# Second LayerNorm of a fused two-layer graph kernel: its row statistics by bn_stats and bn_aggr on VectorE instead of sums on VectorE and squares on ScalarE

## The chip, the cores and the metric

The kernel runs on one core of one Trainium2 chip. The metric is the device time of one execution in microseconds; lower is better. Five engines run their own queues in order and meet at semaphores: TensorE (PE; PEld for its weight loads), VectorE (DVE), ScalarE (ACT), GpSimd (POOL) and SyncE (SP), which issues the DMAs.

## The reference, cut to what matters

```python
# x: (128, 64, 512), adj: (64, 64); weights 512 x 512
def _L1_gnn_ref(h, causal_mask, ...):          # causal_mask = adj
    z_l, z_g, v = h @ W_lang.T, h @ W_grav.T, h @ W_V.T
    zn = z_l / max(norm(z_l), EPS)
    A_l = max(zn @ zn.T, 0) * not_eye
    A_g = exp(-d2(z_g) / (2 * sigma**2)) * not_eye
    K = w_l * row_stochastic(A_l * adj) + (1 - w_l) * row_stochastic(A_g * adj)
    return (K @ v) @ W_O.T
x = _layernorm(x + adj-mixed x + bias)
x = _layernorm(x + _L1_gnn_ref(x, adj, ...))   # the LayerNorm whose statistics change
```

`_layernorm` is (x - mean) / sqrt(var + 1e-5) over the last axis.

## The kernel before

The 128 graphs are worked on in 16 groups of 8. A group is 512 rows, held as four tiles (pairs) of 128 rows x 512 columns, and a name with an index p (`residual(g, p)`) works on one of them. Each engine runs one function `iteration`, once per group, in a fixed order written out by hand: the first group alone, a hardware loop over the next twelve, and the last three alone. What stands in an iteration belongs to several groups at once: the projections of group g (`project`, `diagonal_blocks`, `values`), the Gram matrices of g (`gram`), the attention output of the group before (`attend`, `residual`, the second LayerNorm and the store), the first layer of the next one (`mix`, `add_bias`, `row_stats`, `norm_rows`, `h_high`, `h_low`), and the scaling and splitting of the input of the one after that (`x_scaled`, `x_high`, `x_low`) and of the third (`x_squares`, `x_sum`, `x_base`).

Products run in fp16 with each operand split into a high and a low part. ScalarE makes the high parts (`p_hi`, `u_hi` in `uv`, `h_hi`, `x_hi`, `ks_hi`, `kt_hi`), and VectorE or GpSimd the low ones by subtraction (`p_lo`, `u_lo`, `h_lo`, `x_lo`, `ks_lo`, `kt_lo`).

Names and lines that matter below:

- TensorE: `attend_gate` (L609) is a small matmul in front of `attend` (L628) that carries its waits, among them for `kt_lo` (L1045). `gram` (L552) writes `ps_t`, the four `values` (L538) follow, then `third_norm` (L465), and then `spread` (L567), which needs both halves of `r_sb`: `shifted` (L1064) and `diagonal_matrices` (L1069). `symmetrise` (L576, L578) comes behind it.
- From `ps_t` to `r_sb`: ScalarE copies `t_sb` (`t_copy`, L799), GpSimd makes `t_diag` (L1463), VectorE sums it (`diagonals`, L1056) and scales it (`squared_norms`, nsq, L1060), GpSimd raises it to the power -1/2 (`inverse_norm`, rr, L1469), and VectorE builds `r_sb` from `rr` (L1069).
- GpSimd also subtracts two of the four `h_lo` (L1438, pairs 2 and 3) and all `x_lo` (L1433).
- Second LayerNorm: `residual` (L1120) writes `o` and, as an accumulator output, its row sum `osum`. `out_means` (L1128) turns two sums at a time into `omean`. On ScalarE `o_squares` (L829) squares o plus the mean, and its accumulator is the variance `ovar`. GpSimd's `ln2` (L1446, L1448) makes `rstd2`, VectorE's `out_shift` (L1132) `nmr2`, and ScalarE's `normalise` (L834) writes the output, which SyncE stores.
- `norm_rows` (L1030) overwrites the `h` tile that the residual of the same pair has read, and therefore waits for `sum_ready`, which `residual` raises.
- The last group's statistics (`back`, L1160 on) are bn_stats already.

Of the kernel before, what the change touches and what calls it, by code (L numbers as in the profile page):

```python
# [29 lines left out]
P = 128  # L30
# [28 lines left out]
def resnorm_graph_kernel(nc, x, adj, bias, w_lang, w_grav, w_v, w_o, gate, log_sigma, out):  # L59
# [20 lines left out]
    with ctx:  # L80
# [46 lines left out]
        osum = sb("osum", [P, PAIRS])  # L127
        omean = sb("omean", [P, PAIRS])
        ovar = sb("ovar", [P, PAIRS])
        o_square = sb("o_square", [P, PAIRS, D], BF16)  # L130
# [172 lines left out]
        omean_ready = sem("omean_ready")  # L303
        ovar_ready = sem("ovar_ready")
# [457 lines left out]
        def _(act):  # L762
# [85 lines left out]
            def iteration(g, has_prev, has_next, has_split, has_square):  # L848
# [8 lines left out]
                if has_split and not first:  # L857
                    x_scaled(split, 0)
                    x_scaled(split, 1)
# [4 lines left out]
                if has_split and not first:  # L864
                    x_high(split, 0)
                if has_prev:
                    ks_high(before)
# [3 lines left out]
                if has_split and not first:  # L871
                    x_scaled(split, 2)
                p_high(g, 3, first)
                if first:
                    for p in range(PAIRS):
                        x_scaled(split, p)
                if has_prev:
                    kt_high(before)
                if has_split and not first:
                    x_high(split, 1)  # L880
                p_high(g, 4, first)
                p_high(g, 5, first)
                if has_square:
                    x_squares(third, 0)
                p_high(g, 6, first)
# [4 lines left out]
                if has_next:  # L890
                    if has_square:
                        x_squares(third, 1)
                        x_squares(third, 2)
                    h_high(nxt, 0)
                    if has_prev:
                        u_high(g, 0)
                    if has_split and not first:
                        x_high(split, 2)
                    h_high(nxt, 1)
                    t_copy(g, first)  # L900
                    if first:
                        u_high(g, 0)
                    if has_square:
                        x_squares(third, 3)
                    h_high(nxt, 2)
                    if has_split and not first:
                        x_scaled(split, 3)
                    h_high(nxt, 3)
                    u_high(g, 1)
                    if has_prev:  # L910
                        o_squares(before, 0)
                        o_squares(before, 1)
                        o_squares(before, 2)
                        o_squares(before, 3)
                    u_high(g, 2)
                    if has_split and not first:
                        x_high(split, 3)
                    rectify(g)
# [7 lines left out]
                else:  # L926
                    t_copy(g, False)
                    o_squares(before, 0)
                    o_squares(before, 1)
                    o_squares(before, 2)  # L930
                    o_squares(before, 3)
# [59 lines left out]
        def _(dve):  # L991
# [124 lines left out]
            def residual(g, p, first):  # L1116
                dve.wait_ge(ku_done, g.count(2, p // 2 + 1))
                if p == 0 and not first:
                    dve.wait_ge(o_moved, g.prev().count(16, 32))
                dve.scalar_tensor_tensor(out=o[:, p, :], in0=ku_bank[p][:, :], scalar=ku_scale[:, 0:1],  # L1120
                                         in1=h[g.parity][:, p, :], op0=ALU.mult, op1=ALU.add,
                                         accum_out=osum[:, p:p + 1]).then_inc(sum_ready, 1)

            def out_means(g, half):

                pairs = slice(2 * half, 2 * half + 2)
                dve.wait_ge(sum_ready, g.count(4, 2 * half + 2))
                dve.tensor_scalar(omean[:, pairs], osum[:, pairs], -(D ** -1.5), None, ALU.mult).then_inc(omean_ready, 1)  # L1128

            def out_shift(g):  # L1130
                dve.wait_ge(rstd2_ready, g.count(1, 1))
                dve.scalar_tensor_tensor(out=nmr2[:, :], in0=omean[:, :], scalar=D ** 0.5, in1=rstd2[:, :],  # L1132
# [27 lines left out]
            def back(g):  # L1160
# [15 lines left out]
                def moments(half):  # L1176
                    dve.wait_ge(stats2_ready, 2 * half + 2)
# [28 lines left out]
            def iteration(g, has_prev, has_next, has_split, has_square):  # L1206
# [7 lines left out]
                if has_prev:  # L1214
                    gravities(before)
                    u_low(before, 3)
                    row_sums(before)
                if has_next:
                    add_bias(nxt, 1)
                if has_prev:  # L1220
                    scaled_sums(before)
                    clamped_sums(before)
                if has_next:
                    row_stats(nxt, 0)
                if has_prev:
                    inverse_sums(before)
                    row_factors(before)
# [5 lines left out]
                if has_prev:  # L1233
                    scale_rows(before)
# [4 lines left out]
                if has_prev:  # L1239
                    rows_low(before)  # L1240
                p_low(g, 2)
                if has_next:
                    add_bias(nxt, 2)
                    add_bias(nxt, 3)
                p_low(g, 3)
                if has_next:
                    row_stats(nxt, 2)
# [12 lines left out]
                p_low(g, 6)  # L1260
                p_low(g, 7)
                if has_next:
                    norm_rows(nxt, 0, before)
                    if has_prev:
                        residual(before, 1, False)
                    norm_rows(nxt, 1, before)
# [4 lines left out]
                    h_low(nxt, 0)  # L1271
                    if has_prev:
                        residual(before, 2, False)
                    h_low(nxt, 1)
                    norm_rows(nxt, 2, before)
                    if has_prev:
                        residual(before, 3, False)
                    norm_rows(nxt, 3, before)
                    if has_prev:
                        u_low(g, 0)  # L1280
# [274 lines left out]
```

## Time and profile before

| | us |
|---|---|
| median of three runs | 575.25 |
| the three runs | 574.25, 577.51, 575.25 |
| the profiled execution | 577.62 |
| its span, from first to last instruction | 575.8 |
| TensorE busy in the span | 551.4 (96%) |
| VectorE, ScalarE, GpSimd busy | 466.9, 388.9, 210.8 |
| granted TensorE clock, mean | 0.991 |

All durations in this document come from the profiled execution. A duration in a row runs from start to finish; consecutive operations overlap at their ends, so that the distance between two starts (called the pitch below) is up to 0.1 us shorter. An idle time stands in brackets behind the instruction that it precedes, with what released it.

### The profile page before, as it was taken

The page shows a single profiled execution, that of the slowest core. Times are in us where ns is not written, and L with a number is a line of the kernel's source. Part 1 is how long each engine was busy: PE and PEld are TensorE (multiplying, and loading weights), DVE is VectorE, ACT ScalarE, POOL GpSimd, SP SyncE. Part 2 cuts the span into 40 slices and gives each one's busy share as a digit, 9 for nine tenths or more (in the row PEclk, how much of TensorE's full clock was granted, in tenths as well). Part 3 has the DMA queues.
Part 4 walks back from the last instruction along what each step waited for, and adds up shares of the span by engine and source line. Part 5 has one row for each costly group of instructions (what it writes and reads, how often), then busy time and mean ns, then how long its engine had stood idle before and what let it go on. Part 6 is the DMA issues. An engine that isn't in the chain of part 4 may idle for free.

```text
span 575.8 us, 16176 instructions
## 1 busy us (share of the span) xinstructions
PE 551.4 (96%) x6280; PEld 290.9 (51%) x6280; DVE 466.9 (81%) x1009; ACT 388.9 (68%) x794; POOL 210.8 (37%) x230
## 2 busy tenths in 40 slices
PE   9989789999999999999999999999999999999893
PEld 6544544645454545546454545455464545454361
DVE  1676878798897979797988979797979989896645
ACT  2577736778687677777786876777767866636362
POOL 0132442625244252626152442526262534313021
PEclk9999899999999999999999999999999999999998
DMA  8764161565634435454535344354545332414103
GB/s 247 221 142 90 38 119 42 79 168 67 166 63 130 88 95 127 87 146 96 146 69 154 64 125 98 85 138 87 146 95 146 64 106 38 133 26 88 60 2 146
DMA packets 94845, 60.81 MB, mean 106 GB/s; under 512 B 73184, under 2 KB 75232, under 8 KB 94816
## 3 DMA queue, kind: packets, MB, share of 16 engines
q1 hardware_dynamic: 94816, 60.42, 44.4%
q8 instruction: 19, 0.31, 0.2%
q14 instruction: 10, 0.08, 0.0%
HBM read 21.27 MB, written 16.78 MB: 66 GB/s over the span
## 4 chain that ended last, share of the span: by engine, by line
PE 82%; SPq 6%; DVE 5%; DMA 4%; issue 1%; ACT 1%; POOL 0%; POOLq 0%; ACTq 0%; DVEq 0%
PE proj L538 21%; PE proj L497 18%; PE ps_t L552 8%; PE ps_k L538 7%; PE ps_k L497 6%; PE proj L508 4%; PE front L459 3%; PE ps_v L567 3%; PE ps_t L576 3%; PE ps_k L508 2%; SPq L361 2%; DMA o<-in_L_gnn_W_O 2%; PE ps_t L628 2%; PE front L628 2%; SPq L372 1%
## 5 line engine op out<-in xcount | busy, mean ns | idle before, releaser
L1433 POOL TENSOR_TENSOR x_lo<-x_in,x_hi 128x512 f16<-128x512 f32 x60 | 70.1, 1180 | 158.3 <-ACT x_hi L778 158.3
L538 PE MATMUL proj<-m_hi,ht_hi 128*64 128x512 f16 x384 | 73.8, 381 | 0.0
L538 PE MATMUL proj<-m_hi,ht_lo 128*64 128x512 f16 x384 | 73.4, 379 | 0.0
L538 PE MATMUL proj<-m_lo,ht_hi 128*64 128x512 f16 x384 | 73.4, 379 | 0.0
L1050 DVE TENSOR_TENSOR p_lo<-proj,p_hi 128x512 f16<-128x512 f32 x96 | 63.0, 683 | 9.1 <-ACT p_hi L788 8.0
L788 ACT ACTIVATE p_hi<-proj 128x512 f16<-128x512 f32 x96 | 53.4, 597 | 20.1 <-PE proj L508 20.1
L497 PE MATMUL proj<-ht_lo,l_lang_hi 128*128 128x512 f16 x144 | 54.7, 380 | 2.2 <-DMA ht_lo<-h_lo 1.7
L552 PE MATMUL ps_t<-ht_hi,p_hi 128*128 128x64 f16 x512 | 48.9, 196 | 3.8 <-DVE p_lo L1050 3.8
L1463 POOL TENSOR_TENSOR t_diag<-t_sb,eye 128x512 f32<-128x512 f32 x15 | 19.7, 1310 | 87.4 <-ACT t_sb L799 87.4
L782 ACT ACTIVATE h_hi<-h 128x512 f16<-128x512 f32 x64 | 39.5, 624 | 18.1 <-DVE h L1030 17.9
L552 PEld LDWEIGHTS ps_t<-ht_hi,p_hi 128*128 128x128 f16 x512 | 46.2, 100 | 10.5 <-issue 6.3
L1030 DVE TENSOR_SCALAR h<-y,mv,rstd 128x512 f32<-128x512 f32 x64 | 46.9, 739 | 4.3 <-POOL rstd L1421 1.4
L552 PE MATMUL ps_t<-ht_lo,p_hi 128*128 128x64 f16 x512 | 48.7, 196 | 0.0
L552 PE MATMUL ps_t<-ht_hi,p_lo 128*128 128x64 f16 x512 | 48.7, 196 | 0.0
L508 PE MATMUL proj<-ht_turn,l_turn 64*64 64x512 f16 x288 | 47.3, 380 | 0.0
L552 PEld LDWEIGHTS ps_t<-ht_lo,p_hi 128*128 128x128 f16 x512 | 46.3, 100 | 0.7 <-issue 0.7
L552 PEld LDWEIGHTS ps_t<-ht_hi,p_lo 128*128 128x128 f16 x512 | 46.3, 100 | 0.0
L834 ACT ACTIVATE o<-o,nmr,rstd 128x512 f32<-128x512 f32 x60 | 44.1, 803 | 1.2 <-DVE nmr L1132 0.8
L999 DVE SCALAR_TENSOR_TENSOR y<-front,xinv,bias_b 128x512 f32<-128x512 f32 x60 | 43.1, 739 | 0.2 <-PE front L459 0.2
L829 ACT ACTIVATE o_square<-o,omean 128x512 bf16<-128x512 f32 x60 | 42.5, 710 | 0.0
L1018 DVE BATCH_NORM_STATS2 stats<-y 128x6 f32<-128x512 f32 x64 | 42.1, 682 | 0.0
L772 ACT ACTIVATE x_in<-x_in,xscale 128x512 f32<-128x512 f32 x60 | 41.3, 714 | 0.0
(272 smaller groups left out, 1614.2 us busy)
## 6 DMA issues: line engine op xcount, KB each, us to landing
x_in<-in_x SPq DMA_DIRECT2D x32, 512.0 KB, 7.1
out<-o SPq DMA_DIRECT2D x15, 1024.0 KB, 5.1
ht_turn<-ht_hi SPq DMA_DIRECT2D x16, 192.0 KB, 2.6
ht_turn<-ht_hi SPq DMA_DIRECT2D x16, 128.0 KB, 2.4
w_raw_lang<-in_L_gnn_W_lang SPq DMA_DIRECT2D x4, 256.0 KB, 3.6
o<-in_L_gnn_W_O SPq DMA_DIRECT2D x1, 1024.0 KB, 10.8
w_raw_grav<-in_L_gnn_W_grav SPq DMA_DIRECT2D x4, 256.0 KB, 10.9
uv<-in_L_gnn_W_V SPq DMA_DIRECT2D x1, 1024.0 KB, 15.3
```

Of the source, the lines that this page charges most:

```text
L497: pe.matmul(unit_bank[j][:, :], a[s][:, blk(k, c), :], b[g.parity][:, k, :], start=(n == 0), stop=False, skip_group_check=True)
L508: return pe.matmul(unit_bank[4 * side + c][cols, :], w, x, start=False, stop=True, skip_group_check=True)
L538: mm = pe.matmul(value_bank[p][q * N:(q + 1) * N, :], a[g.parity][:, k, rows:rows + N], b[:, k, :], start=(n == 0), stop=(n == len(passes) ...
L552: mm = pe.matmul(ps_t[:, b * N:(b + 1) * N], a[:, c, b, :, :].rearrange("p s n -> p (s n)"), t[g.parity][:, c, b * N:(b + 1) * N], start=( ...
L788: act.activation(p_hi[:, j % 4, :, j // 4, :], by_batch(unit_bank[j]), ACT.Copy).then_inc(phi_ready, 1)
L829: act.activation(o_square[:, p, :], o[:, p, :], ACT.Square, scale=D ** -0.5, bias=omean[:, p:p + 1], accum_out=ovar[:, p:p + 1]).then_inc( ...
L834: act.activation(o[:, p, :], o[:, p, :], ACT.Identity, scale=rstd2[:, p:p + 1], bias=nmr2[:, p:p + 1]).then_inc(out_ready, 1)
L999: dve.scalar_tensor_tensor(out=y[:, MIXED[p], :], in0=front[p % 2][:, :], scalar=xinv[g.parity][:, 0:1], in1=bias_b[:, :], op0=ALU.mult, o ...
L1018: dve.bn_stats(stats1[:, MIXED[p], :], y[:, MIXED[p], :]).then_inc(stats1_ready, 1)
L1030: dve.tensor_scalar(h[g.parity][:, p, :], y[:, p, :], mv1[:, p, 0:1], rstd1[:, p:p + 1], ALU.subtract, ALU.mult).then_inc(h_ready, 1)
L1050: dve.tensor_tensor(p_lo[:, j % 4, :, j // 4, :], by_batch(unit_bank[j]), p_hi[:, j % 4, :, j // 4, :], ALU.subtract).then_inc(plo_ready, 1)
L1433: pool.tensor_tensor(x_lo[:, p, :], x_in[g.parity][:, p, :], x_hi[:, p, :], ALU.subtract).then_inc(xlo_ready, 1)
```

## The change

The second LayerNorm of all groups but the last gets its statistics as the last group has them. `residual` no longer writes row sums; one `bn_stats` per pair (`out_stats`) reads `o`, and four `bn_aggr` (`out_moments`) make mean and variance. A tiny operation (`hold`) stands between them, as in the first LayerNorm. `out_means` and `o_squares` go. `ln2` and `out_shift` read `mv2`.

```diff
@@ ScalarE @@
-            def o_squares(g, p):
-                act.wait_ge(omean_ready, g.count(2, p // 2 + 1))
-                act.activation(o_square[:, p, :], o[:, p, :], ACT.Square, scale=D ** -0.5, bias=omean[:, p:p + 1],
-                               accum_out=ovar[:, p:p + 1]).then_inc(ovar_ready, 1)
@@ VectorE @@
                 dve.scalar_tensor_tensor(out=o[:, p, :], in0=ku_bank[p][:, :], scalar=ku_scale[:, 0:1],
-                                         in1=h[g.parity][:, p, :], op0=ALU.mult, op1=ALU.add,
-                                         accum_out=osum[:, p:p + 1]).then_inc(sum_ready, 1)
-
-            def out_means(g, half):
-
-                pairs = slice(2 * half, 2 * half + 2)
-                dve.wait_ge(sum_ready, g.count(4, 2 * half + 2))
-                dve.tensor_scalar(omean[:, pairs], osum[:, pairs], -(D ** -1.5), None, ALU.mult).then_inc(omean_ready, 1)
+                                         in1=h[g.parity][:, p, :], op0=ALU.mult, op1=ALU.add).then_inc(sum_ready, 1)
+
+            def out_stats(g, p):
+                dve.wait_ge(sum_ready, g.count(4, p + 1))
+                dve.bn_stats(stats2[:, p, :], o[:, p, :]).then_inc(stats2_ready, 1)
+
+            def out_moments(g):
+                dve.wait_ge(stats2_ready, g.count(4, 4))
+                dve.tensor_scalar(hold[:, :], stats2[:, 0, 0:1], 1.0, None, ALU.mult)
+                for p in range(PAIRS):
+                    dve.bn_aggr(mv2[:, p, :], stats2[:, p, :]).then_inc(mv2_ready, 1)
@@ GpSimd, ln2 @@
-                pool.wait_ge(ovar_ready, g.count(4, 4))
-                pool.tensor_tensor(ve2[:, :], ovar[:, :], eps_ln[:, :], ALU.add).then_inc(ve2_ready, 1)
...
+                inverse_std(g, mv2_ready, mv2, ve2_ready, ve2, rstd2_ready, rstd2)
@@ GpSimd, iteration @@
                 inverse_norm(g)
+                if has_split and not first:
+                    x_low(split, 2)
                 if has_prev:
                     ln2(before)
                 if has_square:
                     x_scale(third)
                     x_back(third)
-                if has_split and not first:
-                    x_low(split, 2)
```

The hand-written orders change with it. On VectorE, ahead of `kt_low`:

```diff
                 if has_prev:
                     gravities(before)
                     u_low(before, 3)
+                if has_next:
+                    add_bias(nxt, 1)
+                if has_prev:
                     row_sums(before)
...
+                if has_prev:
+                    inverse_sums(before)
+                    row_factors(before)
                 p_low(g, 0)
...
+                if has_prev:
+                    scale_rows(before)
                 p_low(g, 1)
+                p_low(g, 2)
+                if has_next:
+                    add_bias(nxt, 2)
                 if has_prev:
                     rows_low(before)
...
                     add_bias(nxt, 3)
+                    row_stats(nxt, 2)
                 p_low(g, 3)
```

Behind the last projections, norm, residual and low parts alternate otherwise: `norm_rows(0)`, `p_low(7)`, `residual(1)`, `h_low(0)`, `norm_rows(1)`, `residual(2)`, `residual(3)`, `norm_rows(2)`, `h_low(1)`, `norm_rows(3)`. No `norm_rows` stands right behind the residual of its own pair any more. `x_inverse` moves behind `similarities`. On ScalarE the input's work (`x_scaled`, `x_high`, `x_squares`) moves: among others the first `x_high` comes behind `p_high(2)`, `x_scaled(1)` ahead of it, and `ks_high` behind it.

VectorE in the loop, from behind the fourth `norm_rows` to `r_sb` from `rr`; register rows are arithmetic of the queue. Before:

```order
L1040 TENSOR_TENSOR uv<-ps_k,uv 128x512
L1128 TENSOR_SCALAR omean<-osum 128x2
L1056 TENSOR_REDUCE diag<-t_diag 128x8
L1060 TENSOR_SCALAR nsq<-diag,eps_nsq 64x8
L1003 REGISTER_ALU
L1005 TENSOR_REDUCE xsum<-xssq 128x1
L1128 TENSOR_SCALAR omean<-osum 128x2
L1064 TENSOR_TENSOR r_sb<-t_sb,diag 64x512
L1039 REGISTER_ALU
L1040 TENSOR_TENSOR uv<-proj0,uv 128x512
L1069 TENSOR_TENSOR r_sb<-eye2,rr 64x512
```

After:

```order
L1105 BN_STATS stats2<-o 128x6
L1019 REGISTER_ALU
L1020 TENSOR_TENSOR uv<-ps_k,uv 128x512
L1036 TENSOR_REDUCE diag<-t_diag 128x8
L1105 BN_STATS stats2<-o 128x6
L1040 TENSOR_SCALAR nsq<-diag,eps_nsq 64x8
L1105 BN_STATS stats2<-o 128x6 x2
L983 REGISTER_ALU
L985 TENSOR_REDUCE xsum<-xssq 128x1
L1044 TENSOR_TENSOR r_sb<-t_sb,diag 64x512
L1049 TENSOR_TENSOR r_sb<-eye2,rr 64x512
```

Ahead of the shift (the `r_sb` from `t_sb`) stand four bn_stats in place of two omeans, and between it and the second `r_sb` the subtraction of `uv` is gone; two of them now stand behind.

GpSimd at the same place, before and after:

```order
L1463 TENSOR_TENSOR t_diag<-t_sb,eye2 128x512
L1437 REGISTER_ALU
L1438 TENSOR_TENSOR h_lo<-h1,h_hi 128x512 x2
L1469 TENSOR_TENSOR rr<-nsq,minus_half 64x8
L1445 REGISTER_ALU
L1446 TENSOR_TENSOR ve2<-ovar,eps_ln 128x4
L1448 TENSOR_TENSOR rstd2<-ve2,minus_half 128x4
```

```order
L1453 TENSOR_TENSOR t_diag<-t_sb,eye2 128x512
L1430 REGISTER_ALU
L1431 TENSOR_TENSOR h_lo<-h1,h_hi 128x512 x2
L1459 TENSOR_TENSOR rr<-nsq,minus_half 64x8
L1426 TENSOR_TENSOR x_lo<-x_in0,x_hi 128x512
L1411 REGISTER_ALU
L1412 TENSOR_TENSOR ve2<-mv2,eps_ln 128x4
L1414 TENSOR_TENSOR rstd2<-ve2,minus_half 128x4
```

An `x_lo` of 128 x 512 elements now stands right behind `rr`, where the two small operations of the second LayerNorm stood.

VectorE in the last group, before and after:

```order
L1056 TENSOR_REDUCE diag<-t_diag 128x8
L1060 TENSOR_SCALAR nsq<-diag,eps_nsq 64x8
L1064 TENSOR_TENSOR r_sb<-t_sb,diag 64x512
L1040 TENSOR_TENSOR uv<-ps_k,uv 128x512
L1069 TENSOR_TENSOR r_sb<-eye2,rr 64x512
L1040 TENSOR_TENSOR uv<-proj0,uv 128x512
L1132 SCALAR_TENSOR_TENSOR nmr2<-omean,rstd2 128x4
```

```order
L1036 TENSOR_REDUCE diag<-t_diag 128x8
L1040 TENSOR_SCALAR nsq<-diag,eps_nsq 64x8
L1044 TENSOR_TENSOR r_sb<-t_sb,diag 64x512
L1105 BN_STATS stats2<-o 128x6 x2
L1109 TENSOR_SCALAR hold<-stats2 128x1
L1111 BN_AGGR mv2<-stats2 128x2 x4
L1020 TENSOR_TENSOR uv<-ps_k,uv 128x512
L1049 TENSOR_TENSOR r_sb<-eye2,rr 64x512
L1020 TENSOR_TENSOR uv<-proj0,uv 128x512
L1115 SCALAR_TENSOR_TENSOR nmr2<-mv2,rstd2 128x4
```

Two bn_stats, the hold and four bn_aggr now stand between the shift and the first `uv`, and so ahead of the second `r_sb`.

## Rows read from the trace of the kernel before

**Rows 1.** The page's first part: busy us (share of the span), instructions.
```profile
PE 551.4 (96%) x6280; PEld 290.9 (51%) x6280; DVE 466.9 (81%) x1009; ACT 388.9 (68%) x794; POOL 210.8 (37%) x230
```

**Rows 2.** Windows: one loop period, us, busy us of each engine, clock, DMA.
```profile
223.62:255.38 31.76, 31.60 (x384) 16.47 (x385) 27.92 (x60) 23.89 (x51) 13.34 (x15) 1.00 0.46 109
```

**Rows 3.** Timeline of PE: start us, us, engine, line, operation, [idle before <-releaser].
```profile
238.34 0.38 PE L538 MATMUL proj<-m_hi,ht_lo 128*64 128x512 f16 x2
238.65 0.18 PE L465 MATMUL front<-xsum,ones 128*128 128x1 bf16 x1
238.69 1.10 PE L567 MATMUL ps_v<-r_sb,w_spread 128*128 128x512 f32 x2
...
254.84 0.38 PE L508 MATMUL proj<-ht_hi,l_grav_lo 64*64 64x512 f16 x1
255.38 0.17 PE L609 MATMUL ps_v<-ones 128*128 128x1 bf16 x1 [0.16 <-DVE kt_lo L1045]
```

**Rows 4.** Groups by line: the squares on ScalarE, busy us, mean ns | idle.
```profile
L829 ACT ACTIVATE o_square<-o,omean 128x512 bf16<-128x512 f32 x60 | 42.5, 710 | 0.0
```

**Rows 5.** Timeline of DVE in the same period.
```profile
227.90 0.08 DVE L1120 DVE_READ_ACCUMULATOR o<-front,ku_scale,h 128x1 f32 x1
228.02 0.55 DVE L1030 TENSOR_SCALAR h<-y,mv,rstd 128x512 f32<-128x512 f32 x1
...
231.48 0.08 DVE L1120 DVE_READ_ACCUMULATOR o<-ps_v,ku_scale,h 128x1 f32 x1
231.67 1.42 DVE L1030 TENSOR_SCALAR h<-y,mv,rstd 128x512 f32<-128x512 f32 x1
...
233.62 0.52 DVE L1128 TENSOR_SCALAR omean<-osum 128x2 f32<-128x2 f32 x1
...
234.76 0.49 DVE L1060 TENSOR_SCALAR nsq<-diag,eps_nsq 64x8 f32<-64x8 f32 x1
...
237.00 0.68 DVE L1069 TENSOR_TENSOR r_sb<-eye,rr 64x512 f32<-64x512 f32 x1 [0.17 <-POOL rr L1469]
```

**Rows 6.** Timeline of POOL beside it.
```profile
231.54 1.27 POOL L1463 TENSOR_TENSOR t_diag<-t_sb,eye 128x512 f32<-128x512 f32 x1 [6.08 <-ACT t_sb L799]
232.77 2.46 POOL L1438 TENSOR_TENSOR h_lo<-h,h_hi 128x512 f16<-128x512 f32 x2
235.33 1.63 POOL L1469 TENSOR_TENSOR rr<-nsq,minus_half 64x8 f32<-64x8 f32 x1
```

**Rows 7.** Timeline of DVE up to L609, then of POOL beside ks_lo.
```profile
241.55 0.68 DVE L1076 TENSOR_TENSOR a_sb<-e_sb,ps_v 64x512 f32<-64x512 f32 x1 [1.42 <-ACT e_sb L803]
...
249.70 1.23 DVE L1114 TENSOR_TENSOR ks_lo<-ks_sb,ks_hi 128x512 f16<-128x512 f32 x1 [0.23 <-ACT ks_hi L813]
...
253.37 1.27 DVE L1018 BATCH_NORM_STATS2 stats<-y 128x6 f32<-128x512 f32 x2
...
254.74 0.41 DVE L1045 TENSOR_TENSOR kt_lo<-ps_v,kt_hi 128x256 f16<-128x256 f32 x1
255.07 0.37 DVE L1023 BATCH_NORM_AGGREGATE mv<-stats 128x2 f32<-128x6 f32 x4
...
249.22 1.16 POOL L1433 TENSOR_TENSOR x_lo<-x_in,x_hi 128x512 f16<-128x512 f32 x1 [7.07 <-ACT x_hi L778]
```

**Rows 8.** Timeline of DVE, then POOL, in the first group.
```profile
73.69 1.55 DVE L1064 TENSOR_TENSOR r_sb<-t_sb,diag 64x512 f32<-64x512 f32 x1
...
72.41 2.27 POOL L1438 TENSOR_TENSOR h_lo<-h,h_hi 128x512 f16<-128x512 f32 x2 [2.35 <-ACT h_hi L782]
```

**Rows 9.** Timeline of DVE, then PE, in the last group.
```profile
552.74 0.69 DVE L1064 TENSOR_TENSOR r_sb<-t_sb,diag 64x512 f32<-64x512 f32 x1
...
554.96 0.68 DVE L1069 TENSOR_TENSOR r_sb<-eye,rr 64x512 f32<-64x512 f32 x1
...
555.29 0.38 PE L538 MATMUL proj<-m_hi,ht_lo 128*64 128x512 f16 x2
555.74 1.10 PE L567 MATMUL ps_v<-r_sb,w_spread 128*128 128x512 f32 x2
```

More of the change, by code:

```diff
@@ L871, in iteration @@
                 if has_split and not first:
-                    x_scaled(split, 2)
+                    x_scaled(split, 1)
+                    x_high(split, 0)
+                if has_prev:
+                    ks_high(before)
                 p_high(g, 3, first)
@@ L876, in iteration @@
                         x_scaled(split, p)
+                if has_split and not first:
+                    x_high(split, 1)
                 if has_prev:
                     kt_high(before)
-                if has_split and not first:
-                    x_high(split, 1)
                 p_high(g, 4, first)
                 p_high(g, 5, first)
+                p_high(g, 6, first)
                 if has_square:
                     x_squares(third, 0)
-                p_high(g, 6, first)
+                    x_squares(third, 1)
                 p_high(g, 7, first)
@@ L890, in iteration @@
                 if has_next:
-                    if has_square:
-                        x_squares(third, 1)
-                        x_squares(third, 2)
                     h_high(nxt, 0)
+                    if has_split and not first:
+                        x_scaled(split, 2)
                     if has_prev:
@@ L1220, in iteration @@
                 if has_prev:
-                    scaled_sums(before)
-                    clamped_sums(before)
+                    row_sums(before)
                 if has_next:
@@ L1225, in iteration @@
                 if has_prev:
-                    inverse_sums(before)
-                    row_factors(before)
+                    scaled_sums(before)
+                    clamped_sums(before)
                 if has_next:
@@ L1260, in iteration @@
                 p_low(g, 6)
+                if has_next:
+                    norm_rows(nxt, 0, before)
                 p_low(g, 7)
                 if has_next:
-                    norm_rows(nxt, 0, before)
                     if has_prev:
                         residual(before, 1, False)
+                    h_low(nxt, 0)
                     norm_rows(nxt, 1, before)
@@ L1304, in iteration @@
                     residual(before, 3, False)
-                    out_means(before, 0)
-                    out_means(before, 1)
+                    out_stats(before, 0)
+                    out_stats(before, 1)
                     dve.wait_ge(t_ready, g.count(1, 1))
@@ L1312, in iteration @@
                     shifted(g)
+                    out_stats(before, 2)
+                    out_stats(before, 3)
+                    out_moments(before)
                     u_low(g, 0)
@@ L1496, in iteration @@
                 inverse_norm(g)
+                if has_split and not first:
+                    x_low(split, 2)
                 if has_prev:
```

69 lines of the change are left out of this document (24 added, 45 removed).

## The prediction

> **What bounds the kernel now.** I read the page's busy shares first: TensorE is busy 551.4 of 575.8 us [rows 1]. Then one period of the loop, cut at the start of the small matmul L609 that gates the attend products: it is 31.76 us long, with TensorE busy 31.60, VectorE 27.9, ScalarE 23.9, GpSimd 13.3, at the full clock [rows 2]. So a period is TensorE's work plus small holes, and the others count only where TensorE waits for them. One such place inside the loop is L609, which the timeline has idle before it for kt_lo [rows 3]. Going by starts, the last products before L609 start at 254.84 and L609 at 255.38, 0.54 us apart, where the two last groups of a period without the wait stand 0.31 apart (the last values product at 238.34, the next matmul at 238.65). So 0.23 us of each period is lost to VectorE's kt_lo, which ends at 254.74 + 0.41 = 255.15 [rows 7]. The other place that matters is spread (L567): it starts at 238.69, right behind its neighbour, and its last input, r_sb, was ready at 237.00 + 0.68 = 237.68 [rows 3, 5]. It has 1.0 us in hand.
>
> **What the change removes.** ScalarE loses four squares per group, 4 x 0.71 = 2.8 us [rows 4]. It is busy 24 of 31.76 us, and TensorE waits for nothing behind the squares, so on the path this is worth nothing. VectorE loses two small omean operations, of which the first takes 0.52 us beside GpSimd [rows 5], and the accumulator reads of the residuals (0.08), which overlap the next instruction.
>
> **What it adds.** VectorE gets four bn_stats, one hold and four bn_aggr per group. Two bn_stats take 1.27 us together, so their pitch is 0.60; four bn_aggr take 0.37, and hold adds under 0.1 [rows 7]. Together 2.8 us, less some 0.5 for the omeans: +2.3 us, VectorE at 30.2 of 31.76. It fits, with 1.5 us of slack in place of 3.8. The waits of the small chain behind it (nmr, the norm of o, the store) have nobody on TensorE behind them. What decides is where the additions stand against the two places above. All times below count from L609 = 0 of a period (223.62 in the trace).
>
> **Step 1, kt_lo.** From a_sb (241.55) to kt_lo (254.74) VectorE needs 13.19 us [rows 7], of which 0.23 is a wait for ks_hi, and ks_lo takes 1.23, some 0.55 more than other operations of its size (0.68 for r_sb, [rows 5]): x_lo runs on GpSimd from 249.22 to 250.38. The new order puts ks_lo behind two more operations, so that the wait for ks_hi goes, and x_lo starts some 1.2 us later against the chain, behind the later x_hi of ScalarE: x_lo now ends about 0.15 us after ks_lo's start, so ks_lo takes 0.8. Against that p_lo 0 now stands ahead of ks_sb and waits about 0.8 us for its p_hi (before 0.2), and x_inverse stands behind a_sb, hidden by the wait for the exponent. Net: 13.07, kt_lo 0.12 us earlier against TensorE, and 0.11 of the 0.23 is left. **-0.12 us a period.**
>
> **Step 2, norm_rows 3 against t_diag.** In the trace t_diag starts on GpSimd at 7.92 (231.54) and the fourth norm_rows at 8.05 (231.67), and takes 1.42 instead of 0.54 us: it waits until the other is nearly through [rows 5, 6]. In the new order the same 13 instructions run ahead of it, but no norm_rows stands right behind the residual it waits for. That wait was 0.12 + 0.20 us (228.02 behind 227.90, 231.67 behind 231.48, beside the pitch). So it starts 0.32 us earlier against p_lo 4, and because L609 itself comes 0.12 sooner, at about 7.85. VectorE is first, by 0.07 us, and keeps its 0.54. t_diag then waits for it and ends at 9.5 instead of 9.19.
>
> **Step 3, r_sb.** bn_stats 0 and u_low 0 fill the time to 9.52; diagonals to 10.25; bn_stats 1 to 10.86; nsq is held until GpSimd's second h_lo ends, as in the trace (234.76 + 0.49 against 232.77 + 2.46), at 11.78. From there VectorE has two bn_stats (1.21), xsum (0.07) and the shift (0.7) before the diagonal matrices: 13.7. GpSimd runs rr from 11.86, 1.63 us, and now has x_lo 2 right behind it: from 13.45 to 14.61. x_lo is first by a quarter of a microsecond, so the diagonal matrices are held. The one row of this kind is the first group's shift, another two-input operation on 64 partitions: 1.55 instead of 0.69 us, ending 0.56 us after h_lo on GpSimd ends (72.41 + 2.27 against 73.69 + 1.55) [rows 8]. So r_sb is ready at 14.61 + 0.56 = 15.17, and spread can start 0.10 later (the last group's latency, 554.96 + 0.68 to 555.74 [rows 9]), at 15.27 instead of 15.07. **+0.20 us a period**, up to +0.35 if GpSimd needs 0.1 more between rr and x_lo; x_base and the two u_low that stand behind r_sb end at 16.9 and are wanted by TensorE from 18.2 on.
>
> [...]
>
> **Step 4, the ends.** In the last group before, r_sb starts at 554.96 behind a u_low that waited for ScalarE's squares, ends at 555.64, and spread starts at 555.74, already 0.14 late (its slot is 555.29 + 0.31) [rows 9]. After: the shift at 552.74, two bn_stats to 554.67, hold and bn_aggr to 555.20, u_low to 555.80, r_sb to 556.48, spread at 556.58. **+0.8 us**, and all that follows is a chain. The first group's m_low is moved by one norm: +0.1.
>
> **The sum.** 13 groups have the x_lo behind rr: 13 x (0.20 - 0.12) = 1.0, 13 x 0.02 for the hidden waits that become exposed = 0.3, and 0.9 at the ends: +2.2 us. The profiled execution took 577.62 us (575.8 of span and 1.8 around it), 2.4 above the median of 575.25, which lies within the spread of three runs. On the profiled one that is 579.8, on the median **577.5 us**.
>
> **Rivals.**
> - *t_diag wins the race of step 2.* My lead is 0.07 us, from pitches read to 0.01 over 13 instructions. If GpSimd is first, norm_rows 3 takes 1.4 again, VectorE is 0.9 late at 9.4, the diagonals start at 10.6, nsq ends at 12.1 and x_lo at 14.9; r_sb is ready at 15.5 and spread starts at 15.6: +0.5 to +0.6 a period, less 0.12: 13 x 0.42 + 0.9 = +6.4, 581.7 us, slower. It decides from 0.07 us of delay before 7.92. For it: in the period shown GpSimd is first. Against: the 0.32 us are plain in the rows.
> - *The diagonal matrices are not held*, because x_lo comes over 0.3 us later than I have it or because this form does not wait. Then r_sb is ready at 14.4, step 3 costs nothing and step 1 stays: -13 x 0.12 + 0.9 = -0.7, 574.6 us. Against: rows 8.
> - *VectorE is simply full.* Every further 0.1 us on VectorE between t_diag and r_sb, or on bn_stats (at a pitch of 0.64 in place of 0.60), adds about 0.06 a period; with four such, +3 us more: 580.5. The Trainium skill (Perfetto Trace Analysis, Optimizing Scalar/DVE Operations) advises moving work from a saturated VectorE to ScalarE, which speaks against this direction; the trace has VectorE below saturation, and by that advice alone the time could only rise.
> - *bn_stats waits for GpSimd too.* Two of the four stand beside h_lo. At 0.8 us each that is 1.6 a period, some +20 us. No row bears it out; 2 in 100, outside the range.
> - A gain of over 0.5% would need more than the 0.23 x 13 = 3.0 us that TensorE waits for kt_lo, all of it and no loss at the end.
>
> **How the numbers follow.** Forecast as summed (+0.5 to +4): 55 in 100. Race lost: 22. VectorE full: 7. Not held: 12. bn_stats held: 2. A gain that I do not see: 2. About 0.5% (2.9 us) is what a measurement of this kernel can tell from no change. Of the forecast's 55 a fifth (11) lies above 578.1; with the race, the full engine and the held bn_stats that makes slower 42. Faster is the 2, and 1 of the not-held case by scatter of the medians: 3. The rest, 55, is no change. The range takes in the not-held case at the low end (574.6, less a little for the median's scatter) and the lost race with its upper bound at the high: 574.0 to 583.0.
>
> **What would show it.** Period 31.8 to 31.9 us. Right if the diagonal matrices take 1.4 to 1.6 us and TensorE waits about 0.2 for them before spread; if norm_rows 3 takes 0.54 and t_diag 1.6; if the wait before L609 halves; and if the last spread comes 0.8 us later after its gate. Wrong if the matrices take 0.68 (then the period falls to 31.64), or if norm_rows 3 still takes 1.4 (period 32.2).

## The result, and the profile after

| | before | after |
|---|---|---|
| median, us (13 runs each) | 576.32 | 579.43 |
| lowest and highest run | 574.25, 580.17 | 577.60, 580.80 |
| profiled execution, its span | 577.62, 575.8 | 578.08, 576.3 |
| period, gate to gate (mean of 11, from the second gate to the thirteenth) | 31.75 | 31.93 |

The ratio is 1.0047, with a 95% interval from 1.0029 to 1.0065: the change costs 2.7 us, between 1.7 and 3.7. (The two medians of the table lie 3.1 apart, inside that interval.) Predicted were 2.2 us; the 577.5 of the prediction stood on a median of 575.25 for the kernel before, which thirteen runs put at 576.32. Against the 0.5% named in the prediction that is no change; the interval says that the loss is real.

The profiled executions lie only 0.5 us apart, because of the start of the program: the first Gram product came 63.0 us into the span before and 61.9 after, and 65.1 in a repeat of the kernel before. That part scatters from run to run, so the traces are compared from place to place in what follows.

First the page of the kernel after, then the windows view over the period that answers to [rows 2] (length, busy us of PE, PEld, DVE, ACT, POOL, clock, DMA):

```profile
PE 553.5 (96%) x6280; PEld 292.7 (51%) x6280; DVE 493.1 (86%) x1054; ACT 347.7 (60%) x674; POOL 210.0 (36%) x230
```
```profile
221.91:253.85 31.94, 31.73 (x384) 16.55 (x385) 29.66 (x63) 21.10 (x42) 13.35 (x14) 1.00 0.46 109
```

ScalarE lost 41 us over the span and nobody gained by it. VectorE has 29.66 instead of 27.92 a period, where I had 30.2. A held instruction counts as busy: the fourth norm_rows and ks_lo are held 0.87 and 0.44 us less, the diagonal matrices and nsq 0.85 and 0.54 more, and the rest of the difference is spread over small instructions.

The timeline of PE in that period, at spread and at the next gate, answers to [rows 3]:

```profile
236.63 0.38 PE L532 MATMUL proj<-m_hi,ht_lo 128*64 128x512 f16 x2
236.94 0.18 PE L459 MATMUL front<-xsum,ones 128*128 128x1 bf16 x1
237.33 0.67 PE L561 MATMUL ps_v<-r_sb,w_spread 128*128 128x512 f32 x1 [0.21 <-issue]
...
253.46 0.38 PE L502 MATMUL proj<-ht_hi,l_grav_lo 64*64 64x512 f16 x1
...
253.85 0.17 PE L603 MATMUL ps_v<-ones 128*128 128x1 bf16 x1
```

Spread now starts 0.39 us behind its neighbour, where it was 0.04. L603, the gate, starts 0.39 behind the last projection, where L609 was 0.54. Over the 13 groups the two sum to +4.6 and -1.9 us. In the last of the 13, behind the loop, spread alone is 0.52 later. The list of waits (us in total, times, longest) has a new row after, and a row of before is gone from it; the new one first, then the old:

```profile
PE ps_v L561 <- issue: 3.6, 14, 0.8
```
```profile
PE ps_v L609 <- DVE kt_lo L1045: 2.0, 12, 0.2
```

The timeline of DVE (VectorE) from the fourth norm_rows to the diagonal matrices, answering to [rows 5]; then POOL (GpSimd) beside it, to [rows 6]. The gate is at 221.91:

```profile
229.75 0.55 DVE L1010 TENSOR_SCALAR h<-y,mv,rstd 128x512 f32<-128x512 f32 x1
230.20 0.69 DVE L1105 BATCH_NORM_STATS2 stats<-o 128x6 f32<-128x512 f32 x1
...
231.47 0.69 DVE L1036 TENSOR_REDUCE diag<-t_diag 128x8 f32<-128x512 f32 x1
232.07 0.68 DVE L1105 BATCH_NORM_STATS2 stats<-o 128x6 f32<-128x512 f32 x1
232.67 1.03 DVE L1040 TENSOR_SCALAR nsq<-diag,eps_nsq 64x8 f32<-64x8 f32 x1
233.62 1.27 DVE L1105 BATCH_NORM_STATS2 stats<-o 128x6 f32<-128x512 f32 x2
...
234.98 0.69 DVE L1044 TENSOR_TENSOR r_sb<-t_sb,diag 64x512 f32<-64x512 f32 x1
235.70 1.53 DVE L1049 TENSOR_TENSOR r_sb<-eye,rr 64x512 f32<-64x512 f32 x1
```
```profile
229.83 1.60 POOL L1453 TENSOR_TENSOR t_diag<-t_sb,eye 128x512 f32<-128x512 f32 x1 [6.48 <-ACT t_sb L793]
231.39 2.29 POOL L1431 TENSOR_TENSOR h_lo<-h,h_hi 128x512 f16<-128x512 f32 x2
233.78 1.63 POOL L1459 TENSOR_TENSOR rr<-nsq,minus_half 64x8 f32<-64x8 f32 x1
235.38 1.30 POOL L1426 TENSOR_TENSOR x_lo<-x_in,x_hi 128x512 f16<-128x512 f32 x1
```

The fourth norm_rows starts 0.08 us ahead of t_diag and keeps its 0.55; t_diag takes 1.60. The diagonal matrices start 0.32 behind x_lo, and take 1.53 instead of 0.68; they end at 237.23, 0.55 after x_lo's end, and spread follows 0.10 later. The bn_stats run beside t_diag and beside h_lo and take 0.69 and 0.68; the mean of all 60 is 680 ns. The Trainium skill (SBUF — State Buffer, Who interferes with whom) leaves VectorE instructions with at most one SBUF input out of the contention with GpSimd, unless they run in a 2-port perf mode, which tensor_scalar can enter. For bn_stats the trace agrees (665 to 699 ns for all 60).

In the two groups behind the loop norm_rows leads by only 0.01 us (in the first of them it starts at 485.28), and there it is held in the changed kernel too: 1.57 and 1.56 us, and t_diag takes 1.27.

Finally the last group, DVE, then PE, answering to [rows 9]:

```profile
552.46 0.69 DVE L1044 TENSOR_TENSOR r_sb<-t_sb,diag 64x512 f32<-64x512 f32 x1
553.18 1.29 DVE L1105 BATCH_NORM_STATS2 stats<-o 128x6 f32<-128x512 f32 x2
...
555.43 0.67 DVE L1049 TENSOR_TENSOR r_sb<-eye,rr 64x512 f32<-64x512 f32 x1
...
555.01 0.38 PE L532 MATMUL proj<-m_hi,ht_lo 128*64 128x512 f16 x2
556.21 1.10 PE L561 MATMUL ps_v<-r_sb,w_spread 128*128 128x512 f32 x2 [0.81 <-issue]
```

Spread comes 1.20 behind its neighbour instead of 0.45: +0.75 us.

### The profile page after: what moved, and what is told of

The parts are those of the page before. It is cut to its first block, busy times and chain, and to the rows that moved or that the text cites. A ratio compares the mean times of both kernels' runs of the same rounds, so it can differ in the third digit from the quotient of the medians.

```text
span 576.3 us, 16089 instructions
## 1 busy us (share of the span) xinstructions
PE 553.5 (96%) x6280; PEld 292.7 (51%) x6280; DVE 493.1 (86%) x1054; ACT 347.7 (60%) x674; POOL 210.0 (36%) x230
## 4 chain that ended last, share of the span: by engine, by line
PE 93%; DVE 4%; issue 1%; ACT 1%; POOL 0%; POOLq 0%; ACTq 0%; DVEq 0%
PE proj L532 22%; PE proj L491 19%; PE ps_t L546 9%; PE ps_k L532 8%; PE ps_k L491 6%; PE front L453 4%; PE proj L502 4%; PE ps_v L561 3%; PE ps_t L570 3%; PE ps_k L502 3%; PE proj L743 2%; PE ps_t L622 2%; PE front L622 2%; PE ps_t L502 1%; PE ps_v L591 1%
## 5 line engine op out<-in xcount | busy, mean ns | idle before, releaser
L1426 POOL TENSOR_TENSOR x_lo<-x_in,x_hi 128x512 f16<-128x512 f32 x60 | 73.2, 1223 | 117.1 <-ACT x_hi L772 117.1
L1030 DVE TENSOR_TENSOR p_lo<-proj,p_hi 128x512 f16<-128x512 f32 x96 | 64.3, 685 | 14.8 <-ACT p_hi L782 14.8
L782 ACT ACTIVATE p_hi<-proj 128x512 f16<-128x512 f32 x96 | 52.0, 599 | 25.5 <-PE proj L502 25.5
L1453 POOL TENSOR_TENSOR t_diag<-t_sb,eye 128x512 f32<-128x512 f32 x15 | 23.4, 1557 | 93.1 <-ACT t_sb L793 93.1
L797 ACT ACTIVATE e_sb<-ps_t 64x512 f32<-64x512 f32 x16 | 9.5, 592 | 67.5 <-PE ps_v L572 67.5
L787 ACT ACTIVATE uv<-proj 128x512 f16<-128x512 f32 x48 | 28.4, 592 | 25.8 <-PE proj L532 25.8
L998 DVE BATCH_NORM_STATS2 stats<-y 128x6 f32<-128x512 f32 x64 | 43.4, 684 | 0.0
L766 ACT ACTIVATE x_in<-x_in,xscale 128x512 f32<-128x512 f32 x60 | 42.7, 717 | 0.0
```

Of the source, the lines that this page charges most:

```text
L766: act.activation(x_in[g.parity][:, p, :], x_in[g.parity][:, p, :], ACT.Copy, scale=xscale[g.parity][:, 0:1]).then_inc(xscaled_ready, 1)
L782: act.activation(p_hi[:, j % 4, :, j // 4, :], by_batch(unit_bank[j]), ACT.Copy).then_inc(phi_ready, 1)
L998: dve.bn_stats(stats1[:, MIXED[p], :], y[:, MIXED[p], :]).then_inc(stats1_ready, 1)
L1030: dve.tensor_tensor(p_lo[:, j % 4, :, j // 4, :], by_batch(unit_bank[j]), p_hi[:, j % 4, :, j // 4, :], ALU.subtract).then_inc(plo_ready, 1)
L1426: pool.tensor_tensor(x_lo[:, p, :], x_in[g.parity][:, p, :], x_hi[:, p, :], ALU.subtract).then_inc(xlo_ready, 1)
```

## The experiments

Six of the nine experiments are single runs. The 13 runs of the kernel before lie up to 6 us apart, so for a single run the trace decides and not its time.

**The kernel before once more.** It tells what two traces of one kernel differ by.

> The kernel before, once more, to see what its first 80 us and its last two groups do from one execution to the next. Loop period 31.76 us again by every theory. In the changed kernel's profile three stretches were shorter than in the first profile of before: 1.1 and 1.8 us on loads before the first projection, 0.5 us before the last group's first projection. If these are scatter of the DMA, this profile shows other numbers there; if the change brought them, it shows 2.1 and 0.7 us gaps again.

Measured: 578.94 us in one run, periods of 31.76. The first Gram product came 2.1 us later than in the other trace, and the stretch from there to the second group's first projection took 18.9 instead of 19.7 us; in the kernels with the new order it took 18.5 to 19.0. What the traces differ by ahead of the loop is therefore no evidence. The wait ahead of the last group's first projection is another matter: it came again (the projection starts 0.75 us behind its neighbour, 0.68 in the first trace, 0.15 after), and is counted below. A place that does scatter is a stretch ahead of the last group's Gram product. Windows view, in the kernel before, after, and in the next experiment (the clock is the third number from the end):

```profile
544.95:546.66 1.71, 1.71 (x3) 0.49 (x2) 0.44 (x4) 0.00 (x0) 0.00 (x0) 0.50 0.00 0
```
```profile
544.67:546.07 1.40, 1.40 (x4) 0.34 (x2) 1.40 (x3) 0.00 (x0) 0.00 (x0) 0.61 0.00 0
```
```profile
541.63:542.49 0.86, 0.86 (x4) 0.29 (x2) 0.86 (x3) 0.00 (x0) 0.00 (x0) 1.00 0.00 0
```

The granted clock there was 0.50 (the lower level, 1.2 GHz), 0.61 and 1.00 (2.4 GHz) for the same products, and it goes with no edit: four of eleven traces pass the place in 0.86 us, among them kernels of the old order and of the new. So neither the 0.31 us between before and after at this place nor the 0.85 of the next kernel is a result. In the Gram products behind it the kernel after gives some 0.26 of the 0.31 back.

**GpSimd's x_lo back at its old place.** The changed kernel with one edit:

```diff
@@ GpSimd, iteration @@
                 inverse_norm(g)
-                if has_split and not first:
-                    x_low(split, 2)
                 if has_prev:
                     ln2(before)
                 if has_square:
                     x_scale(third)
                     x_back(third)
+                if has_split and not first:
+                    x_low(split, 2)
```

> The changed kernel with one part undone: on GpSimd x_low(split, 2) stands behind x_back again, not behind rr. Theory A (that x_lo holds the diagonal matrices): the matrices take 0.68 us, TensorE's gap before spread is 0.04 again, the wait before L603 stays at 0.39 between starts, period 31.94 - 0.34 = 31.6 us, the last group unchanged; time 13 x 0.34 = 4.4 us under the changed kernel, about 575.0, 0.3% under the kernel before. Theory B (VectorE is too full after t_diag, whatever GpSimd does): the gap before spread stays near 0.3, time as the changed kernel, 579.

Measured: 575.56 us (12 runs), ratio to before 0.9973 (0.9950 to 0.9995). Its timeline of DVE and its windows view:

```profile
235.52 0.68 DVE L1049 TENSOR_TENSOR r_sb<-eye,rr 64x512 f32<-64x512 f32 x1
```
```profile
221.73:253.33 31.60, 31.60 (x384) 16.48 (x385) 28.87 (x63) 21.07 (x42) 13.19 (x14) 1.00 0.46 110
```

The matrices take 0.68 and the period is all TensorE. From 1.0047 to 0.9973 are 4.3 us; the trace has 13 times 0.34 = 4.4. Theory A held. The whole loss of the loop, and more than the whole loss of the change, is this one GpSimd instruction. What stays (four bn_stats a group and the new order) is faster than before by 0.3% (0.05 to 0.5%).

**The same move in the kernel before**, with no bn_stats added:

> The kernel before, with one edit: GpSimd's x_lo of pair 2 stands right behind rr, as in the change. Theory A (whoever starts first on the two-input path holds the other, so the x_lo behind rr is what holds the diagonal matrices): the matrices take 1.4 to 1.6 us here as well, without any bn_stats; rr ends near 13.1 to 13.3 from the gate, so r_sb is ready near 14.9 to 15.0 and spread, whose slot is 15.07, loses 0 to 0.1. Period 31.76 to 31.85. Theory B (the matrices are held because the new statistics delay VectorE into GpSimd's way): they take 0.68 here, period 31.76.

Measured: 577.40 us in one run, period 31.82. DVE, then POOL, with the gate at 224.22:

```profile
236.03 1.67 DVE L1064 TENSOR_TENSOR r_sb<-t_sb,diag 64x512 f32<-64x512 f32 x1
237.73 0.69 DVE L1040 TENSOR_TENSOR uv<-proj,uv 128x512 f16<-128x512 f32 x1
238.34 0.92 DVE L1069 TENSOR_TENSOR r_sb<-eye,rr 64x512 f32<-64x512 f32 x1
```
```profile
235.94 1.63 POOL L1469 TENSOR_TENSOR rr<-nsq,minus_half 64x8 f32<-64x8 f32 x1
237.54 1.18 POOL L1433 TENSOR_TENSOR x_lo<-x_in,x_hi 128x512 f16<-128x512 f32 x1
```

The hold appears without the statistics. The matrices take 0.92 us, not 1.4 to 1.6 as I wrote, because they start 0.80 behind x_lo, where it was 0.32; but they end 0.54 after x_lo's end, as after the change. They start that late because the shift ahead of them is held as well, which neither theory had. It takes 1.67 us in all 12 groups of the loop. In the kernel before it takes 0.69:

```profile
235.42 0.69 DVE L1064 TENSOR_TENSOR r_sb<-t_sb,diag 64x512 f32<-64x512 f32 x1
```

In both kernels the shift starts 0.09 us behind rr, and rr takes 1.63. What differs is the x_lo queued behind rr, and the held shift ends 0.13 after rr's end. Why a queued x_lo should matter before it has started is open.

Spread is ready just past its slot and loses 0.07. The move alone costs 0.07 a period; in the new kernel, where rr ends 0.15 later, after a later nsq, and x_lo meets the end of the shift and takes 1.30, it costs 0.34.

**The statistics made short.** The changed kernel with bn_stats over 8 of the 512 columns; the second LayerNorm's statistics are in effect left out:

```diff
-                dve.bn_stats(stats2[:, p, :], o[:, p, :]).then_inc(stats2_ready, 1)
+                dve.bn_stats(stats2[:, p, :], o[:, p, 0:8]).then_inc(stats2_ready, 1)
```

> The changed kernel with the four bn_stats of the second LayerNorm over 8 of 512 columns (its statistics are left out in effect), so that VectorE has about 2 us less in each group, all else the same. Theory A: nsq still ends with the second h_lo, x_lo still starts ahead of the diagonal matrices, now at most 0.1 us, and they are held still: 1.6 us, gap before spread 0.25 instead of 0.38, period 31.83. Theory B: the gap before spread is 0.04 and the period 31.6. The last spread comes 0.75 us earlier by both (two full bn_stats ahead of the last matrices are gone).

Measured: 580.22 us in one run, period 32.08: with 2.1 us less work on VectorE in each group its period is longer than the full kernel's 31.93. Theory B missed. Of theory A the hold came (1.63 us, the matrices 0.06 behind x_lo), but not the times: spread starts 0.53 behind its neighbour, where it was to have a gap of 0.25. In the last group spread came 0.74 us earlier, as both had it, so those two bn_stats are step 4's loss. DVE, then POOL, with the gate at 223.35:

```profile
233.64 0.39 DVE L1040 TENSOR_SCALAR nsq<-diag,eps_nsq 64x8 f32<-64x8 f32 x1
...
234.25 1.41 DVE L1044 TENSOR_TENSOR r_sb<-t_sb,diag 64x512 f32<-64x512 f32 x1
237.19 1.63 DVE L1049 TENSOR_TENSOR r_sb<-eye,rr 64x512 f32<-64x512 f32 x1 [1.53 <-POOL rr L1459]
```
```profile
232.83 2.28 POOL L1431 TENSOR_TENSOR h_lo<-h,h_hi 128x512 f16<-128x512 f32 x2
235.06 2.10 POOL L1459 TENSOR_TENSOR rr<-nsq,minus_half 64x8 f32<-64x8 f32 x1
237.13 1.15 POOL L1426 TENSOR_TENSOR x_lo<-x_in,x_hi 128x512 f16<-128x512 f32 x1
```

VectorE comes to the shift early, while h_lo still runs; the shift waits for it (1.41), and ends at 235.66. That lies in rr, which takes 2.10 instead of 1.63. So rr ends 13.81 from the gate instead of 13.50, x_lo starts at 13.78 instead of 13.47, and the matrices end 0.54 after it. In the full kernel bn_stats 1 delays nsq past the end of the first h_lo, nsq is then held to the end of the second, two more bn_stats follow, and the shift starts 1.30 behind h_lo's end. The work that I had counted as a burden keeps two operations apart.

**The race of step 2, lost.** The changed kernel with a small VectorE operation (128 columns) ahead of the fourth norm_rows:

```diff
                     h_low(nxt, 1)
+                    if has_prev:
+                        dve.tensor_scalar(late[:, :], bias_b[:, 0:128], 1.0, None, ALU.mult)
                     norm_rows(nxt, 3, before)
```

> The change plus one small VectorE operation (0.1 to 0.2 us, 128 columns) ahead of the fourth norm_rows, so that t_diag starts first. If the lead of 0.08 us is what protects the norm: the norm takes 1.3 to 1.5 us, t_diag falls from 1.6 to about 1.3, diagonals start about 1.0 later, spread starts 0.3 to 0.4 later than in the changed kernel, period 32.2 to 32.3, about +4 us. If the order of starts does not matter: the norm keeps 0.55, the extra 0.1 to 0.2 us hides, period 31.94 to 32.0.

Measured: 580.08 us in one run, period 32.14. DVE, then POOL:

```profile
231.76 1.50 DVE L1011 TENSOR_SCALAR h<-y,mv,rstd 128x512 f32<-128x512 f32 x1
```
```profile
231.70 1.28 POOL L1456 TENSOR_TENSOR t_diag<-t_sb,eye 128x512 f32<-128x512 f32 x1 [6.48 <-ACT t_sb L794]
...
235.85 1.63 POOL L1462 TENSOR_TENSOR rr<-nsq,minus_half 64x8 f32<-64x8 f32 x1 [0.45 <-DVE nsq L1041]
```

GpSimd is first by 0.06 us and VectorE is held: 1.50. The matrices end 15.53 from the gate, and spread comes 0.59 behind its neighbour: +0.55 against before, as rival 1 had it (0.5 to 0.6). Against the changed kernel it is +0.21 a period, 2.7 us, and not the 4.2 between my two totals, because the forecast case was itself dearer than I had it. The expectation above (0.3 to 0.4 later, period 32.2 to 32.3) is missed. The norm, t_diag and the diagonals, 1.0 us later, came as it says, but nsq now comes behind both h_lo and takes 0.21 us instead of the held 1.03, so that it ends only 0.21 later.

**The statistics back on ScalarE, in the new order**, with GpSimd's old order. Of the change only the moved lines are left. The edit of the two orders, without the last group's lines; on ScalarE u_high 2 also comes ahead of the last x_high:

```diff
@@ VectorE, against the changed kernel @@
-                        out_stats(before, 0)
                         u_low(g, 0)
+                        out_means(before, 0)
                     diagonals(g)
-                    if has_prev:
-                        out_stats(before, 1)
...
-                    if has_prev:
-                        out_stats(before, 2)
-                        out_stats(before, 3)
                     if has_square:
                         x_sum(third)
+                    if has_prev:
+                        out_means(before, 1)
                     shifted(g)
...
-                        out_moments(before)
@@ ScalarE @@
                     u_high(g, 1)
+                    if has_prev:
+                        o_squares(before, 0)
+                        o_squares(before, 1)
+                        o_squares(before, 2)
+                        o_squares(before, 3)
                     u_high(g, 2)
```

> The new order of VectorE, ScalarE and GpSimd's old order, but with the second LayerNorm's statistics as before (accumulated sums on VectorE, squares on ScalarE). Theory A (the gain ahead of the gate comes from the order, and the statistics themselves cost and bring nothing): gap before the gate 0.38 in place of 0.54, no gap before spread, period 31.60, about 575.0 us, the same as the change with GpSimd's old order. Theory B (ScalarE's relief by 2.8 us a group is what makes kt_lo earlier): the gap stays 0.54, period 31.76, about 576.7.

Measured: 575.36 us (12 runs), ratio 0.9966 (0.9939 to 0.9993), period 31.60, 0.39 before the gate. It is as fast as the version with bn_stats (the intervals overlap almost wholly): the gain at the gate is the order's, and in the loop the statistics cost and bring nothing. Which of the moved lines, VectorE's or ScalarE's, makes the gain was not tried apart. The kernel also has a case of the race that I had not ordered, DVE, then POOL:

```profile
229.18 1.58 DVE L1030 TENSOR_SCALAR h<-y,mv,rstd 128x512 f32<-128x512 f32 x1
```
```profile
229.21 1.27 POOL L1464 TENSOR_TENSOR t_diag<-t_sb,eye 128x512 f32<-128x512 f32 x1 [6.48 <-ACT t_sb L799]
```

VectorE starts 0.03 us ahead and is held all the same. With 0.08 of a lead in the changed kernel it was not: the race turns between the two. Here the lost race costs nothing: the matrices wait for rr, are not held, and spread keeps its 0.04.

**How full VectorE is.** GpSimd's old order, and two or four more bn_stats a group into a tile that nobody reads. The edit for two; for four it is range(4):

```diff
                     if has_prev:
                         out_moments(before)
+                        for p in range(2):
+                            dve.bn_stats(extra[:, p, :], o[:, p, :])
                     if has_square:
                         x_base(third, x_norm_bank)
```

> The change with GpSimd's old order and two more bn_stats per group (into a tile that nobody reads) behind the four bn_aggr: 1.21 us more on VectorE, at about 29.5 + 1.2 of 31.6 us busy. Theory A (only the place counts; VectorE has 1.22 us of wait ahead of a_sb and the u_low are 1.5 us early there): the wait for e_sb goes to about 0, period stays 31.60 to 31.65. Theory B (VectorE is full): every added microsecond there shows in the period at once, 32.0 or more.

> As the run with two more bn_stats, but with four (2.4 us more on VectorE in every group, behind the four bn_aggr). The run with two kept the period at 31.60 and had no wait left ahead of a_sb, so this one should show where VectorE becomes the bound: if every microsecond beyond that slack counts, a_sb starts 1.1 to 1.3 us later after the gate, TensorE waits 1.1 to 1.3 us longer before the next gate, period 32.7 to 32.9, about +14 us over the run with two. If there is still slack further on in the chain to kt_lo, less than 0.3.

Measured, one run each: 574.38 us with two, period 31.60; 581.78 with four, period 32.15. The windows view of the first:

```profile
221.17:252.78 31.61, 31.60 (x385) 16.46 (x385) 30.61 (x65) 21.09 (x42) 13.20 (x14) 1.00 0.47 110
```

So VectorE can be busy 30.61 of 31.61 us and cost nothing, as theory A had it; the third rival is out. With four, the second 1.2 us cost 0.55, half of what I wrote, and not where I wrote it. The gap before the gate stays 0.38, since a_sb comes 1.15 later but a wait of 0.59 for p_hi further on swallows half of it, and the rest is no more than what TensorE has lost elsewhere by then. TensorE waits instead in symmetrise (0.4 a period) and, in every second group, in the products behind it (0.2), for x_base, which stands behind the added work. From the list of waits, and the timeline of DVE:

```profile
PE ps_t L571 <- DVE xbase L990: 2.8, 12, 0.2
```
```profile
240.31 0.13 DVE L990 TENSOR_SCALAR xbase<-front 128x1 f32<-128x1 f32 x1
```

**A version that beats both.** GpSimd's old order, and in the last group the statistics of pairs 2 and 3 ahead of the shift, the moments behind the matrices:

```diff
@@ VectorE, last group @@
-                    shifted(g)
                     out_stats(before, 2)
                     out_stats(before, 3)
+                    shifted(g)
+                    diagonal_matrices(g)
                     out_moments(before)
                     u_low(g, 0)
-                    diagonal_matrices(g)
```

> As the first (GpSimd's old order), and in the last group VectorE does bn_stats 2 and 3 ahead of the shift, then the diagonal matrices, and bn_aggr and u_low behind them. Step 4 right: rr is no longer met by the shift and takes 1.63 instead of 2.13, the matrices start 1.0 us earlier than in the changed kernel, the last spread starts in its slot 0.31 behind the last product (1.19 in the changed kernel), 0.8 to 0.9 us less than the first of these kernels: about 574.2, 0.4% under the kernel before. If the end of the program does not hang on that spread, no difference between the two.

Measured: 575.11 us (12 runs), ratio 0.9962 (0.9937 to 0.9988). PE in the last group:

```profile
552.91 0.38 PE L532 MATMUL proj<-m_hi,ht_lo 128*64 128x512 f16 x2
553.23 1.12 PE L561 MATMUL ps_v<-r_sb,w_spread 128*128 128x512 f32 x2
```

Spread starts 0.32 behind its neighbour: the two bn_stats run while rr is made, and the 0.75 us are gone. By the trace the gates give 2.0, the last group's first projection 0.5 and the end 0.1 against before, and the first projections of the second and third groups lose 0.6 in waits for transposed rows: 2.0 us, and 2.2 were measured. By its time it can't be told apart from the kernel with only x_lo moved back (0.9962 and 0.9973, with intervals that overlap); that the last spread's delay is gone is shown by the trace.

## Why the prediction was right, step by step

The place-to-place comparison gives 4.57 (spread, 13 groups) - 1.93 (gates) - 0.07 (second group's first projection) - 0.52 (the last group's) + 0.75 (last spread) = +2.8 us, against 2.7 measured and 2.2 predicted. The period came to 31.93, just over the 31.8 to 31.9 of the prediction.

- **Step 1** said that kt_lo comes 0.12 earlier and 0.11 of the wait stays: the gap fell by 0.15, from 0.54 to 0.39. No wait is left that the list shows, but 0.08 over the 0.31 without a wait is, and the gate still starts 0.22 behind kt_lo's end (0.23 before). ks_lo took the 0.8 of the prediction, in place of the 1.23 of [rows 7]; in both it ends 0.55 after x_lo's end. The experiments without the x_lo, with short statistics or with the squares on ScalarE have the same gap, so it is the order.

```profile
249.87 0.79 DVE L1094 TENSOR_TENSOR ks_lo<-ks_sb,ks_hi 128x512 f16<-128x512 f32 x1
...
253.22 0.41 DVE L1025 TENSOR_TENSOR kt_lo<-ps_v,kt_hi 128x256 f16<-128x256 f32 x1
```

- **Step 2** held to 0.01 us: norm_rows at 7.84 from the gate (7.85), t_diag at 7.92 to 9.52 (9.5). But the rival's condition was too kind. I let VectorE win by any lead; with 0.03 it loses. The lead came to 0.08, of which the race needs more than 0.03, so the margin was under 0.05 us, thinner than the 0.07 that I gave it. In the two groups behind the loop the lead was 0.01 and the race was lost, which the prediction did not look at.
- **Step 3** is the term that was mis-sized. nsq ended at 11.79 (11.78) and rr started at 11.87 (11.86). x_lo started at 13.47 (13.45) but took 1.30, not 1.16: it met the end of the shift, which I had placed on VectorE at this very time (up to 13.7) without asking what it does to x_lo. The matrices ended at 15.32 (15.17), spread 15.42 (15.27), against the 15.07 before. That is 0.34 a period where the forecast had 0.20 + 0.02, the 0.02 without a row behind it. It lies inside the 0.35 that was kept, but that was kept for a gap between rr and x_lo, which did not come.
- **Step 4**: +0.75 for +0.8. The +0.1 for the first group's m_low can't be read: it lies in the part that scatters.
- **Not foreseen**: 0.52 us less at the last group's first projection, which before waited for transposed rows of h_lo. The last h_lo ends 11.6 us behind the gate ahead of it in both kernels, but the last transpose lands at 16.96 instead of 17.61. The wait is also gone without the x_lo behind rr, with the late norm and in the best version; it is there with short statistics (17.77) and with the squares on ScalarE (17.64), which have the new order too. So the order alone does not explain it, and the cause is open.
- **Luck in the total**: step 3 cost 1.7 us more than forecast (4.6 for 2.9). The 0.52, 0.07 at the second group's first projection, 0.4 more at the gates and 0.2 less at the ends hide all but 0.6 of it. The path and the sign were right by the mechanism; that 2.2 lies so near to 2.7 owes something to errors that cancel.
- The rivals: the matrices were held in 13 of 13 groups; VectorE had 1.2 us a period to spare; bn_stats is not held by GpSimd. A gain of over 0.5% was to need more than all of kt_lo's wait: the best version has 0.4%.

## What to carry to other kernels

List side by side, by starting times, the instructions of VectorE and GpSimd that were seen to hold each other (here GpSimd's t_diag, h_lo and x_lo against VectorE's two-input operations on SBUF and its tensor_scalar, not its bn_stats or what reads PSUM): of a pair that overlaps one waits for the other in most cases, and what counts is which of them the path runs through. The shift beside rr, held in one kernel and not in the other, says that such a list needs a trace for each new order. Of an edit that moves many lines, price each engine's moves alone; here one GpSimd line cost 4.3 us and the rest gained 1.6. Harmless work between two of the critical operations can be worth more than the gap it fills.

## What the runs showed of the hardware that was not expected

- In recorded starts a lead of 0.01 us (changed kernel, behind the loop) or of 0.03 (squares on ScalarE) does not save norm_rows from being held; one of 0.08 does.
- An operation held by t_diag, h_lo or x_lo ends at a fixed distance from the other's recorded end, whatever its own start: the matrices 0.55, 0.54, 0.54 and 0.55 us (after, moved x_lo in the old kernel, short statistics, late norm), norm_rows 0.28 in all cases.
- The shift, starting 0.09 us behind rr, takes 0.69 where ve2 stands behind rr and 1.67 where x_lo does, before that x_lo has started.
- GpSimd's power on 64 x 8 is lengthened too, where the shift started first: 2.10 beside the held shift, 1.63 otherwise. The large subtraction is, by 0.14 us, where it starts 0.3 ahead of the shift's end.
- nsq, an operation on 64 x 8, takes 0.21 us alone and 1.03 beside h_lo; it ends with the first of the two h_lo if it comes before that one's end (0.39), otherwise with the second.
